# Two panels of codes and a ring of ten strips, in place of three and six, in a fused two-layer graph network

## The reference

```python
deg = jnp.maximum((adj != 0).astype(jnp.float32).sum(-1), 1.0)
# layer 0
pooled = dinv * (adj + eye) * dinv @ x + x          # dinv = rsqrt(deg)
x = _layernorm(x + relu(pooled @ W + b))
# layer 1
type_sum = adj @ x
attn_a, attn_b = sigmoid([type_sum, x] @ Wa.T + ba), sigmoid([type_sum, x] @ Wb.T + bb)
h = x @ W_sa
e = where(adj != 0, exp(-leaky_relu(s_left[:, None] + s_right[None, :], 0.01)), 0)
x_a = (e / (sum(e, axis=1) + 1e-05)) @ h
x_b = adj @ (x @ W_gcnb) + b_gcnb
out = _layernorm(x + sigmoid(attn_a * x_a + attn_b * x_b))
```

## Time and profile before

| what | value |
|---|---|
| median of 3 runs | 872.14 us (871.7 to 872.2) |
| the profiled execution | 871.72 us, of which the span of its instructions is 869.6 us |
| PE busy in the span | 852.1 us (98%) |
| granted clock of TensorE, mean | 0.999 |
| DMA issues of strips | 128, 512 KB each, 7.2 us from issue to landing (median) |
| DMA issues of codes | 16, 1024 KB each, 8.4 us (median) |

### The profile page before, as it was taken

The page is one execution under the profiler, slowest core; times in us unless marked ns, Lnnn a source line. Parts: engine busy times, 40 slices in busy tenths (PEclk is TensorE's granted clock), DMA queues, the critical chain, the costliest instruction groups (busy, mean ns, idle before and its releaser), DMA issues.

```text
span 869.6 us, 20453 instructions
## 1 busy us (share of the span) xinstructions
PE 852.1 (98%) x7574; PEld 753.9 (87%) x7574; DVE 668.7 (77%) x1180; ACT 574.2 (66%) x1217; POOL 181.2 (21%) x181
## 2 busy tenths in 40 slices
PE   8999989999999998999999999999999999999997
PEld 7888878888888887888888888888888888888886
DVE  5697666665656467899988988987978978978863
ACT  4765555555554337989976976876976966967831
POOL 1002223222322221012222022122032032032031
PEclk9999999999999999999999999999999999999999
DMA  9889989999999733110221121120120120220001
GB/s 313 277 269 348 341 293 386 338 336 354 320 339 369 269 137 144 56 52 6 79 81 29 50 78 34 45 78 24 54 78 24 54 78 6 72 78 0 26 25 37
DMA packets 66649, 130.01 MB, mean 150 GB/s; under 512 B 5496, under 2 KB 29088, under 8 KB 62112
## 3 DMA queue, kind: packets, MB, share of 16 engines
q1 hardware_dynamic: 57392, 120.61, 39.0%
q10 hardware_dynamic: 9200, 8.64, 3.0%
HBM read 99.87 MB, written 29.36 MB: 149 GB/s over the span
## 4 chain that ended last, share of the span: by engine, by line
PE 74%; DVE 10%; issue 6%; DMA 4%; ACT 4%; POOL 1%; SPq 1%; ACTq 0%; DVEq 0%; POOLq 0%
PE ps L1576 27%; PE ps L1417 21%; PE ps L1517 18%; PE ps L1452 4%; DMA strip<-in_adj_dram 3%; DVE ec L1142 2%; DVE em L1149 2%; PE ps L1399 2%; ACT ec L640 2%; DMA xs<-in_x_dram 1%; ACT em L649 1%; DVE dd L968 1%; PE ps L1437 1%; DVE sc L824 1%; PE ps L1384 0%
## 5 line engine op out<-in xcount | busy, mean ns | idle before, releaser
L1576 PE MATMUL ps<-fb,em 128*128 128x257 f16 x3072 | 347.5, 273 | 0.8 <-DVE em L1149 0.8
L1576 PEld LDWEIGHTS ps<-fb,em 128*128 128x128 f16 x3072 | 300.4, 98 | 38.6 <-issue 1.3
L1417 PE MATMUL ps<-y,codes 128*128 128x257 f16 (+1 forms) x2048 | 237.0, 273 | 0.0
L1417 PEld LDWEIGHTS ps<-y,codes 128*128 128x128 fp8e4 x2048 | 200.2, 98 | 25.9 <-DVE y L857 0.4
L640 ACT ACTIVATE ec<-slb,nsb 128x256 f32<-128x256 f32 x512 | 211.1, 497 | 0.0
L1149 DVE SCALAR_TENSOR_TENSOR em<-ec,em 128x2048 f16<-128x2048 f32 x64 | 147.4, 2303 | 20.4 <-ACT em L649 20.4
L649 ACT ACTIVATE em<-ec 128x2048 f16<-128x2048 f32 x64 | 122.0, 1908 | 59.8 <-PE ps L1576 50.8
L1142 DVE SCALAR_TENSOR_TENSOR ec<-ec,pan 128x2048 f32<-128x2048 f32 x64 | 147.3, 2302 | 2.3 <-issue 1.8
L515 ACT ACTIVATE codes<-strip 128x1024 uint8<-128x1024 f32 x67 | 69.5, 1050 | 39.0 <-DMA strip<-in_adj_dram 38.3
L1517 PE MATMUL ps<-zz,dd 128*128 128x256 f16 x768 | 89.4, 273 | 0.1
L463 POOL TENSOR_TENSOR sc<-sc,sc 128x2 f32<-128x2 f32 x15 | 36.6, 2440 | 244.6 <-DVE sc L1251 244.6
(11 more groups left out here) (153 smaller groups left out, 781.1 us busy)
## 6 DMA issues: line engine op xcount, KB each, us to landing
strip<-in_adj_dram SPq DMA_DIRECT2D x128, 512.0 KB, 7.2
a_scratch<-codes SPq DMA_DIRECT2D x16, 1024.0 KB, 8.4
pan<-a_scratch SPq DMA_DIRECT2D x16, 1024.0 KB, 4.9
x_scratch<-x ACTq DMA_DIRECT2D x32, 128.0 KB, 5.5
x1r<-x_scratch SPq DMA_DIRECT2D x16, 256.0 KB, 2.7
h_scratch<-hst ACTq DMA_DIRECT2D x30, 136.0 KB, 5.1
out_dram<-ot SPq DMA_DIRECT2D x15, 256.0 KB, 2.2
fb<-h_scratch SPq DMA_DIRECT2D x3, 1088.0 KB, 8.7
```

What stands on the lines that cost most here:

```text
L1417: mm = pe.matmul(ACC(n)[:, 0:cols], codes[:, qq % SLOTS, h, jb, e * P:(e + 1) * P].bitcast(F8), y[:, jb, part, 0:cols], start=(jb == 0 and ...
L1576: mm = pe.matmul(PH(2 * m + e)[:, 0:HC], em[:, c, e_part, i, e * P:(e + 1) * P], fb[:, jb, h_part, 0:HC], start=(jb == 0 and e_part + h_pa ...
```

## The change

`SLOTS` goes from 3 to 2 and `RING` from 6 to 10. The third slot's 16 KB in each partition become the first four places of the ring, so all that lies behind keeps its address. From this follows:

- Strip `s` waits for the cast of strip `s - 10`, in place of `s - 6`.
- A cast of group `qq` waits for the sums and the stored codes of group `qq - 2`, in place of `qq - 3`.
- The codes of group `q` are stored behind strip `16 (q + 2)`, in place of `16 (q + 3) - 6`: group 0 behind strip 32 in place of 42.
- `pan` now lies where the first four places of the ring are. Its first load waits for all casts and the stored codes of group 0, in place of the sums of group 5 and two slots' stores.

```diff
-RING = 6
-SLOTS = 3
+RING = 10
+SLOTS = 2
...
-O_S = O_C + SLOTS * 2 * T * PW
+O_S = O_C + SLOTS * 2 * T * PW + 4 * SJ * 2 * PW * 4
...
-    strip = at("strip", [P, RING, SJ, 2 * PW], F32, O_S)
+    strip = at("strip", [P, RING, SJ, 2 * PW], F32, O_S - 4 * SJ * 2 * PW * 4)
...
-    area = Area(O_S + RING * SJ * 2 * PW * 4, O_L1)
+    area = Area(O_S + (RING - 4) * SJ * 2 * PW * 4, O_L1)
...
-    wabs = at("wabs", [P, KD, D], F32, O_S + RING * SJ * 2 * PW * 4)
+    wabs = at("wabs", [P, KD, D], F32, O_S + (RING - 4) * SJ * 2 * PW * 4)
...
-            CODES_AT = [(q + SLOTS) * GS - RING for q in range(NQ - 2)]
+            CODES_AT = [(q + SLOTS) * GS for q in range(NQ - 2)]
...
             codes_when_cast(NQ - 2)
-            last = (NQ - 3) % SLOTS
-            sp.wait_ge(S["acc_done"], PT * (NQ - 2))
-            for slot in (0, last):
-                sp.wait_ge(codes_out[slot], 32 * len(range(slot, NQ - 2, SLOTS)))
+            for sem, n in zip(("cast_act", "cast_dve"), casts_until(NSTRIP - 1)):
+                sp.wait_ge(S[sem], n)
+            sp.wait_ge(codes_out[0], 32)
             for m in range(2):
                 sp.dma_start(pan[:, m], a8d[m]).then_inc(panel_in[m], 16)
```

## The result

| | before | after |
|---|---|---|
| median, lowest to highest, of 6 runs each | 871.92 us (869.46 to 872.54) | 867.15 us (867.05 to 867.54) |
| the profiled execution | 871.72 us | 867.15 us, span 865.0 us |
| granted clock, mean | 0.999 | 0.999 |

The ratio of after to before is 0.9947, 95% interval 0.9934 to 0.9959: 4.8 us faster, between 3.6 and 5.8. The forecast was 868.5, a gain of 3.6.

What follows compares the result with a forecast made beforehand. PE bounds the kernel, busy 852.1 of 869.6 us, with 4.88 us in three gaps before projections. Taking 0.56 and 3.02 from 871.72 gives 868.14, from the median 868.56; predicted 868.5, 80% range 867.0 to 870.3.

Steps and rivals of the forecast that it cites:

- Gap 1: PE's wait at p_step(1), behind landing strip 31: `q` of projection 0 0.56 us earlier, gap from 1.15 to 0.59.
- so no more is to be had: At p_step(1): after the 0.56 us gain the chain from `q` to `x1t_lo` itself is late, leaving 0.59.
- Gap 2: PE's wait at p_step(3): its chain has no DMA and moves as a whole, so it stays at 0.71 us.
- The rival that one cause, too few buffers, stands behind all three gaps: At p_step(1), p_step(3) and p_step(5): ten places cure every gap, 4.88 us less, 867.3; chance 0.10.
- Gap 3: PE's wait at p_step(5), behind late strips 43 to 47: all 3.02 us go, with 2 us or more to spare.
- Only a deeper ring can use those idle shares: DMA share 0.77 at 40 to 60 us, 0.68 at 84 to 92: ring full, SP waiting for a cast.
- The sum: Whole kernel: 871.72 - 0.56 - 3.02 = 868.14; the same step from the median 872.14 gives 868.56, predicted as 868.5.
- the forecast's own case: At p_step(5) and p_step(1): the 3.02 us gap gone, the 1.15 us gap halved, 867.9 to 869.2; chance 0.70.
- The new waits: Casts of group q + 2 wait for group q's stores: group 0's land between 77.7 and 83.4 us; cost taken as nothing.
- the slower rival: First cast of each group from the second on: late stores hold it, 881.5 if they land after 28 us; chance 0.05.
- The load of `pan`: After the last casts: issued at 280.3, landed by 301.0 at latest, read by DVE at 304.7; costs nothing.
- The bandwidth rival: Strips before p_step(5): full DMA engines, not lead, make them late; 870.1 or 871.6; part of the gap staying, chance 0.08.

Runs made afterwards that it cites:

- no_gaps: The changed kernel with DVE's `x1t_lo(1)` and `x1t_lo(3)` moved ahead of `head` and `normalize` of tiles 3 and 5; 866.3 us, ratio 0.994 to before.
- early_no_gaps: The kernel before (three slots, ring of six) with group q's stores behind strip 16(q+2) and `x1t_lo(1)`, `x1t_lo(3)` moved earlier on DVE; 867.37 us, ratio 0.9946.
- late_stores: The changed kernel with each group's stores nine strips later, group 0's behind strip 41; 892.6 us, ratio 1.0249 to before.
- early_stores: The kernel before (three slots, ring of six) with only the stores of group q moved to behind strip 16(q+2); 868.34 us, ratio 0.9959.
- filled_gap: The kernel before with 26 unused PE transposes of the identity ahead of the projection of panel 5; 871.29 us, ratio 0.9999 to before.
- before_fourth: The kernel before, unchanged, profiled a fourth time to see where its runs differ; 872.05 us.

## Why the prediction was right, and where it wasn't

**Gap 1 halved: right, size and reason.** `q` of projection 0 came at 76.12, 1.53 after PE's start (forecast 1.54), and the gap is 0.59 and 0.60 in the two profiles of after. Wrong was "so no more is to be had": with DVE's order changed the gap is gone, with ten places (no_gaps) and with six (early_no_gaps).

**Gap 2 stays: right**, 0.71 or 0.72 in every profile that keeps DVE's order, whatever the ring (but for late_stores, where PE is late already). The rival that one cause, too few buffers, stands behind all three gaps fell, and no_gaps shows what does stand behind the second. By the rule of the Trainium skill's "Perfetto Trace Analysis" (Optimization Strategy, right behind the section that the prediction names), a repeated gap can mean too little memory on the chip; the traces agree for the half of gap 1 that went with eight and ten places, and for the rest of gap 3.

**Gap 3 gone: right as to the kernel, wrong as to the cause.** The step that failed is the sentence "Only a deeper ring can use those idle shares". In early_stores the ring is as before, and yet the share from 84 to 92 us is 1.03 in place of 0.68, and gap 3 is 0.19. The stores' move by ten strips was in my working, but only as a cost to be borne, while it was most of the cure: strip 43 no longer has 2.1 MB of stores right ahead of it at 92.76. In DVE's old order the ring gives the half of gap 1 and the rest of gap 3, and eight places give as much as ten.

**The sum: its two terms right, but not all of the gain.** The forecast of 868.5 was 1.35 above the 867.15 measured, a gain of 3.6 against 4.8. The two profiles differ by 871.72 - 867.15 = 4.57 us, and this is 0.56 and 3.17 of gaps and 1.16 of start, which is chance, less 0.23 given back, 4.66 in all (0.09 more than measured): near 460 us PE waits 1.15 us at line 1516, where it waited 0.92 at 463.46 before. The medians differ for another reason. After's ten runs have a median of 867.17; before's at a clock of 0.998 or more 870.71. That difference is 3.5, near the forecast's 3.6. The rest goes with before's 26 runs at a lower clock, 1.8 us later. So gap 3 may have a second price, that the clock sometimes falls behind it: seen in one profile, agreeing with the 31 runs that have neither gap 3 in full nor the low clock, and not confirmed by filled_gap. That the measured time lies in the range is in part luck: 867.15 is near its lower end of 867.0 and outside the forecast's own case (867.9 to 869.2). By the number alone it is the time of the rival in which all three gaps go (867.3), and only the profile, with gap 1 at 0.59 and gap 2 at 0.71, tells the two apart. I took the profiled execution, at 0.999, as typical of before, and it was one of the minority.

**The new waits: right.** The stores landed before 78, as I took it, and no cast waited for them, with ten places (4 us to spare at strip 32) or with six (0.3). But the threshold and price that I gave the slower rival were too mild: where the stores do come late, all groups pay and the clock falls too (892.6 against the 881.5 that I had worked out for 28 us).

**The load of `pan`: right.** Issued at 278.37 (forecast 280.3), it took 4.8 and 7.0 us, not 14.6 to 20.7, and DVE read it first at 303.34 without a wait.

**The bandwidth rival** fell: the rate was no obstacle, though my picture of the DMA engines was off. I expected a share of 0.77 from 40 to 60 us and one well below 1 from 96 to 116; it was 0.86 and 1.00. The lead of the ring of ten is built up in the one (with early stores and six places it is 0.79), and group 1's stores, at 97.70, fall into the other. A full DMA share is no sign of a late strip; the wait in front of its reader is.

**Left open:** what besides a gap of 2 to 3 us lowers the clock (late_stores has it fall after 2.21 and 2.24 us and not after 3.34), and why each kernel with two slots waits 1.14 to 1.16 us near 460 us and each with three 0.89 to 0.92 (late_stores has no such wait). A ring of ten with the stores at their old place wasn't tried: with three slots the memory is full, and with two, the casts from strip 32 on would wait for stores that stand behind them.

## What to carry to other kernels

Where loads and stores share a queue, look first at where the stores stand: here moving them in one line took 2.8 of the 3.0 us of the longest gap and made the kernel 3.6 us faster by its ratio, while the four more buffers brought 1.2 to 1.8 us, all of it with the first two as far as these runs can tell. Trace each gap's chain by itself: three gaps that looked alike, ahead of the same instruction, had three cures. Gap 3 answered to the stores' place, gap 2 to the order of DVE's steps, and gap 1 by half to the ring and wholly to that order. And look at several executions of the kernel before and at their clocks, before one of them is made the base of a sum.

## What the runs showed of the hardware

- The granted clock falls to 0.50 after a PE gap of 2.94 us in one execution of before and stays at 1.00 after 2.94, 3.02 or 3.06 us in others. In one execution of late_stores it falls after gaps of 2.21 and 2.24 us and stays at 1.00 after one of 3.34. After 5.91 us it fell before PE was back (0.62 from 92 to 94 us of late_stores). Mostly at 0.50 (before_fourth), 16 matmuls took 3.58 us in place of 1.92.
- The DMA engines moved 394 GB/s over 8 us in after, as over 20 us in before. From 96 to 116 us a share near 1 went with 3.7 us of PE idle in before (1.03) and with 0.65 in after (1.00).
- A pair of 1 MB stores that leaves with strips ahead of it in the queue lands after about 12 us (10.6 and 12.8 in after, 11.8 and 14.0 in late_stores); two 1 MB loads of `pan` with a quiet queue take 4.8 to 7.0.
